# A graph network's messages: gathered before they are summed, or scattered in order of dst as they are spread

## What is computed

```python
# layer 0
msgs = edge_weight[:, None] * (h @ w)[src];   agg = segment_sum(msgs, dst)
# layer 1 (from dst to src), gate from edge attributes and node types
msg = gate * h[dst] * (cw * mj)[:, None];     agg = segment_sum(msg, src)
# layer 2, twice
x = segment_sum(x[src] * edge_weight[:, None], dst)
# layer 3, three times
prop = segment_sum(w[:, None] * h[row], col)   # w = -dis[row] * (row != col) * dis[col]
```

## Time and profile before

| what | value |
|---|---|
| median of 3 runs | 21002.24 us (20997.84 to 21006.39) |
| the profiled execution's own time | 21139.88 us |
| its span | 21138.1 us |
| busy PE / DVE / ACT / POOL | 12659.3 / 13740.0 / 5212.8 / 7402.5 us |
| DMA, mean over the span | 212 GB/s |
| written to and read from HBM | 1727.75 MB and 2805.63 MB |

### The profile page before, as it was taken

The page is one execution under the profiler, slowest core; times in us unless marked ns, Lnnn a source line. Parts: engine busy times, 40 slices in busy tenths (PEclk is TensorE's granted clock), DMA queues, the critical chain, the costliest instruction groups (busy, mean ns, idle before and its releaser), DMA issues. The chain is left out here.

```text
span 21138.1 us, 471985 instructions
## 1 busy us (share of the span) xinstructions
PE 12659.3 (60%) x138981; PEld 10558.5 (50%) x140202; DVE 13740.0 (65%) x29579; ACT 5212.8 (25%) x13806; POOL 7402.5 (35%) x7744
## 2 busy tenths in 40 slices
PE   5666666666600476557755675576556556556655
PEld 4555555555500355545544455455545545555555
DVE  8555555555533476679978876677667666666765
ACT  0222222222211354014420450153014104202400
POOL 0555555555554201533310005402520550251054
PEclk7788778788755798568888995698666666666655
DMA  7222222222255599989977896698659659866965
GB/s 275 80 81 81 81 80 81 81 81 80 78 155 120 176 343 334 333 280 340 330 228 231 279 316 182 202 322 267 183 203 407 208 160 358 309 183 237 405 185 145
DMA packets 1900227, 4491.37 MB, mean 212 GB/s; under 512 B 314350, under 2 KB 750924, under 8 KB 1899366
## 3 DMA queue, kind: packets, MB, share of 16 engines
q1 hardware_dynamic: 912598, 1942.76, 28.3%
q0 software_dynamic: 437168, 1300.53, 20.2%
q10 hardware_dynamic: 550368, 1246.92, 15.5%
HBM read 2805.63 MB, written 1727.75 MB: 214 GB/s over the span
## 5 line engine op out<-in xcount | busy, mean ns | idle before, releaser
L1435 POOL DMA_INDIRECT sum_slots<-messages,sum_rows x2820 | 2664.4, 945 | 7504.6 <-ACT sum_rows L1447 5728.8
L1518 PE MATMUL sum_sums<-sum_slots,sum_onehot 128*128 128x144 bf16 (+1 forms) x31584 | 3650.3, 298 | 2616.9 <-DVE sum_onehot L1492 1787.4
L1518 PEld LDWEIGHTS sum_sums<-sum_slots,sum_onehot 128*128 128x128 bf16 x31584 | 3193.7, 132 | 3073.4 <-issue 3073.4
L808 POOL DMA_INDIRECT records<-rec,row_i x3125 | 2992.0, 957 | 2832.8 <-DVE rec L674 2066.3
L728 PE MATMUL ps_l<-place,turned 98*128 98x98 f32 x6250 | 1158.3, 352 | 1725.7 <-ACT place L609 1719.0
L1236 PE MATMUL exp_rows<-tab,h 128*128 x40608 | 1645.6, 191 | 809.1 <-DVE exp_times L1290 500.0
L1242 PE MATMUL exp_rows<-tab,h 128*128 x13536 | 1479.5, 288 | 845.0 <-ACT exp_stage L1373 707.6
L728 PEld LDWEIGHTS ps_l<-place,turned 98*128 98x128 f32 x6250 | 1047.6, 257 | 1802.2 <-issue 1802.2
L1477 DVE TENSOR_REDUCE sum_whole<-sum_sums 128x96 f32<-128x288 f32 (+1 forms) x1974 | 914.8, 463 | 1484.7 <-remote 874.5
L1242 PEld LDWEIGHTS exp_rows<-tab,h 128*128 128x128 bf16 x13536 | 1272.0, 128 | 1052.4 <-issue 1045.2
L1236 PEld LDWEIGHTS exp_rows<-tab,h 128*128 128x128 bf16 x40608 | 1475.6, 98 | 514.8 <-issue 315.0
(11 more groups left out here) (293 smaller groups left out, 22730.8 us busy)
## 6 DMA issues: line engine op xcount, KB each, us to landing
exp_places<-src_places SPq DMA_DIRECT2D x1692, 512.0 KB, 6.1
messages<-exp_stage ACTq DMA_DIRECT2D x1410, 576.0 KB, 11.3
messages_first<-exp_stage ACTq DMA_DIRECT2D x282, 832.0 KB, 7.3
sum_slots<-messages_back SPq DMA_DIRECT2D x282, 600.0 KB, 4.4
messages_back<-fill ACTq DMA_DIRECT2D x624, 270.5 KB
l_places<-dst_places SPq DMA_DIRECT2D x282, 512.0 KB
recc<-records SPq DMA_DIRECT2D x282, 448.0 KB
l_gate<-records SPq DMA_DIRECT2D x282, 448.0 KB
```

The source lines that it names most:

```text
L808: pool.indirect_dma_start(rec_dram, bass.IndirectOffsetOnAxis(ap=row_i[:, g, k:k + 1], axis=0), rec[:, g, k, :], None).then_inc(put[g], 16)
L1435: pool.indirect_dma_start(gath[:, c, g, :], None, of_dram, bass.IndirectOffsetOnAxis(ap=row_g[:, c, g:g + 1], axis=0)).then_inc(g_dma[c], 16)
L1518: last = pe.matmul(sums[:, c % RS, g, 0:3 * width], onehot[:, c % RS, g * B + k, :], of[:, k * 3 * width:(k + 1) * 3 * width], start=(k == ...
```

## The change: what it does

Spreading no longer stores in order; summing no longer gathers. POOL scatters each group of a pair (one indirect DMA per group, L1392 of the changed kernel) to its row in the order of dst while it is spread. Blocks that hold no edge are out of range and dropped, so all three message tensors are zeroed first, in the edge stage. Summing loads rows in order on SP, and PE adds the three bf16 parts itself, by 48 matmuls of 48 columns a pair. `u_dram` is gone; its features stay in `messages_first`. In a weighted unit `less_second` moves on PE's queue to the start of the next unit.

```diff
@@ edge stage
+        zeroed = [d.rearrange("(p n) f -> p (n f)", p=P) for d in (msg0_dram, msg_dram, back_dram)]
...
                             attrs(i, first, g)
+                            sp.dma_start(*piece(i, first, g, 0)).then_inc(s_zero, 16)
...
-                            act.dma_start(to, fill[:, 0:many].bitcast(BF16)).then_inc(s_back, 16)
+                            for k in (1, 2):
+                                act.dma_start(*piece(i, first, g, k)).then_inc(s_back, 16)
@@ block stage
-                        act.copy(sent[:, c % RS, :, 0, :], f[:, :, :, D + SREL])
-                        act.copy(sent[:, c % RS, :, 1, :], f[:, :, :, D + EW])
+                        act.copy(sent[:, c % RS, :, 0:B], f[:, :, :, D + SREL])
+                        act.copy(sent[:, c % RS, :, B:2 * B], f[:, :, :, D + EW])
+                        act.copy(sent[:, c % RS, :, 2 * B], number1[:, at])
...
-                            dve.scalar_tensor_tensor(out=empty[:, :], in0=found[:, :], scalar=0.0, in1=less_big[:, :],
-                                                     op0=ALU.is_equal, op1=ALU.mult).then_inc(s_emp, 1)
-                            dve.wait_ge(s_emp, 2 * n)
-                            dve.tensor_tensor(found[:, :], found[:, :], empty[:, :], ALU.add).then_inc(s_emp, 1)
-                            dve.wait_ge(s_emp, 2 * n + 1)
-                            dve.tensor_tensor(idx_g[:, at], found[:, :], number[:, at], ALU.add).then_inc(s_fnd, 1)
@@ layer 1: the type features are read from the first message tensor
-        u_view = u_dram.rearrange("p (n f) -> p n f", f=B * G)
+        u_view = msg0_dram.rearrange("(g p) f -> p g f", p=P)[:, :, ROW // 2:ROW0 // 2]
@@ expand, PE
                                     if weighted:
+                                        if u >= 3:
+                                            less_second(i, *before(u, 3))
+                                        elif not first:
+                                            less_second(i - 1, *before(u, 3))
 
                                         pe.matmul(unread[:, :], ident_b[:, :], flat[:, 0:512], start=True, stop=True)
...
-                                        for d, step in ((2, less_first), (3, less_second)):
-                                            if u >= d:
-                                                step(i, *before(u, d))
-                                            elif not first:
-                                                step(i - 1, *before(u, d))
+                                        if u >= 2:
+                                            less_first(i, *before(u, 2))
+                                        elif not first:
+                                            less_first(i - 1, *before(u, 2))
@@ expand, ACT
-                                if c >= LAG:
-                                    store(i, c - LAG)
-                                elif not first:
-                                    store(i - 1, RC - LAG + c)
+                                if not first:
+                                    act.wait_ge(x_st[c], i * (16 * CH) + e * (TURNS * 16 * CH))
+                                act.copy(row_d[:, c, :], idx_d[:, bass.ds(i * RG + c * CH, CH)]).then_inc(x_row, 1)
@@ expand, POOL
+                                lone_wait(pool, x_row, i * RC + (e * RC * TURNS + c + 1))
+                                if weighted:
+                                    lone_wait(pool, x_third, i * UT + (bw + (c + 1) * UC))
+                                else:
+                                    for q in range(2):
+                                        lone_wait(pool, x_out[q], i * (UT // 2) + (bo + (c + 1) * (UC // 2)))
+                                for g in range(CH):
+                                    pool.indirect_dma_start(
+                                        to_dram, bass.IndirectOffsetOnAxis(ap=row_d[:, c, g:g + 1], axis=0),
+                                        stage[:, c, g, :], None,
+                                        bounds_check=last_block, oob_is_err=False).then_inc(x_st[c], 16)
@@ collect: gather (POOL), row copies (ACT) and the save of u_dram (SP) are gone
+                                sp.dma_start(slots_in[:, c, :, :],
+                                             in_order[:, bass.ds(i * RG + c * CH, CH), 0:length // 2 if wide else length]
+                                             ).then_inc(g_load[c], 16)
...
-                            dve.tensor_reduce(
-                                whole[:, :, :],
-                                sums[:, c % RS, :, 0:3 * width].rearrange("p g (j f) -> p g f j", j=3),
-                                AX.X, ALU.add).then_inc(g_red, 1)
-                            dve.wait_ge(g_red, i * RC + (bc + c + 1))
...
-                                dve.tensor_tensor(to, to, whole[:, g, :], ALU.add).then_inc(g_acc, 1)
+                                dve.tensor_tensor(to, to, sums[:, c % RS, g, 0:width], ALU.add).then_inc(g_acc, 1)
@@ collect, PE
+                                pe.matmul(unread[:, :], ident_b[:, :], places_flat[:, 0:512], start=True, stop=True)
                                 pe.wait_ge(g_oh, i * RC + (bc + c + 1))
-                                lone_wait(pe, g_dma[c], i * each + (bl + each))
+                                lone_wait(pe, g_load[c], i * 16 + (bl + 16))
                                 if c >= RS or not first:
-                                    lone_wait(pe, g_red, i * RC + (bc + c + 1 - RS))
+                                    lone_wait(pe, g_acc, i * (RC * CH) + (ba + (c + 1 - RS) * CH))
                                 for g in range(CH):
...
                                     for k in range(B):
-                                        last = pe.matmul(sums[:, c % RS, g, 0:3 * width],
-                                                         onehot[:, c % RS, g * B + k, :],
-                                                         of[:, k * 3 * width:(k + 1) * 3 * width],
-                                                         start=(k == 0), stop=(k == B - 1))
+                                        for j in range(3):
+                                            n = k * 3 + j
+                                            last = pe.matmul(sums[:, c % RS, g, 0:width],
+                                                             onehot[:, c % RS, g * B + k, :],
+                                                             of[:, n * width:(n + 1) * width],
+                                                             start=n == 0, stop=n == 3 * B - 1)
```

187 lines of the change are left out of this document (73 added, 114 removed).

## The result

The changed kernel takes **20847.25 us** (median of 4 runs, 20842.81 to 20849.54); the kernel before took 21000.04 us beside it (20997.33 to 21006.39). The ratio is 0.9927, 95% interval 0.9909 to 0.9944. It is faster, as forecast, and the time lies in the range, but of the 489 us that the sum promised 153 came.

A forecast was written before the change was run, and what follows sets the result against it. Mostly nothing was full and engines waited for each other; unweighted spreading was DMA bound. Summing -1463, weighted +734, unweighted 0, edge +250, block -50, rest +40: -489 us, 21002 to 20510 us; range 19600 to 21300.

The forecast's parts named there:

- the scatter itself fits: Weighted spreading: two scatter issues at 1.28 us take 2.55 us of POOL in a pair of 3.4.
- PE becomes the longest: Summing: PE needs 2.1 us a pair, DMA 1.9, DVE 1.66; with gaps at turns, 2.40 us a pair.
- lower bound of 1.9: Summing: at best the DMA's 1.9 us a pair, which would save 990 us more.
- rival D: Summing: gaps at PE's turns and waits overlap, 2.05 us a pair, 690 better, kernel 19820 us; chance 0.11.
- Rival B: Summing: PE's small matmuls limit at 49 ns each, 3.15 us a pair, kernel slower at 22000 us; chance 0.17.
- the loop through POOL and ACT, and the low clock that the gaps bring: Gathered summing: what the change removes, as the gather itself is not slow; pairs go from 3.25 to 2.40 us.
- The price of the order: Weighted spreading: moved less_second waits for ACT's copy, +0.75 us in one unit, +0.10 in the one with the fetch.
- rival A: Weighted spreading: the subtraction's wait falls into PE's idle time, the 734 us go, kernel 19780 us; chance 0.20.
- upper bound of 1270: Weighted spreading: at worst +1.5 us a pair, 0.75 in each unit, +1270 us.
- rival C: Unweighted spreading: scatters keep the gathers' 3.25 us a pair, three stages lose 507, kernel 21020 us; chance 0.10.
- Weighted stages hide it: Weighted spreading: scatters at the gathers' pace of 3.25 us a pair would cost nothing there.
- PE waits for `place` in 469 of 469 rounds, so all of it counts: Edge stage: ACT's second DMA delays place by 0.4 us in each of 625 rounds, +250 us.

The follow-up runs named there:

- e2: Kernel before, stores still in order on ACT's queue, with only the second subtraction moved as the change moves it: 19525.79 us, ratio 1.0569.
- e1: Changed kernel with the weighted spreading's second subtraction put back behind the 24 matmuls, on a faster chip (before: 18480 us): 17208.28 us, ratio 0.9314.
- e9: Changed kernel with the second subtraction put back behind the 24 matmuls, on a slower chip (before: 20993.81 us): 19873.37 us, ratio 0.9466.
- e8: Changed kernel with ACT's two zeroing DMAs of an edge round cut in two each, on a slower chip: 20953.65 us, edge stage 5409.8 us.
- e11: Changed kernel with PE loading spreading window numbers once per turn, not per pair, on a slower chip (before: 21133.04 us): 20977.81 us, ratio 0.9926.
- e12: Changed kernel with the second subtraction back in place and window numbers loaded once per turn, on a slower chip: 20023.69 us, ratio 0.9475.
- e5: Changed kernel with the three unweighted spreadings storing in src order from ACT instead of scattering, on a faster chip: 18006.33 us against the change's 17991.07.

## Why the prediction was wrong

The direction held, and so did the mechanisms named for the two large terms. Two steps failed. One is a cost put at nothing: "the scatter itself fits", worked out from POOL's own time. On the chip that was measured PE's signals come late beside scatters, and the six spreadings lost 2086 us where 734 were forecast. The other is a size: "PE becomes the longest" with 2.40 us a pair of the summing, where 1.95 were measured.

**Summing, -1463, measured -2347.** The miss is the pace after: (2.40 - 1.95) x 1974 pairs = 888 us. 48 matmuls take 1.22 us, not 1.64, and the stage runs at its DMA's pace, just above my lower bound of 1.9. The 34 ns of the earlier trace rows came from a stretch of 0.82 us that had the unread matmul in it. Without its 0.22, which I then added once more, it is 0.60/24 = 25 ns, what the 48 show. That is rival D's outcome, 884 us better than the forecast where I had put it at 690, though D had the gaps overlap and not the matmuls cheaper. Rival B, at 3.15 us a pair, falls. (Its threshold was also added up wrong: 3.14 - 0.49 is 2.65 us a pair, not 2.75.) The page TensorE: Matmul & The Clock Gate of the Trainium skill, section Back-to-back issue gap, gives 81 ns as the sustained spacing of pairs at 128 columns, and its table about 25 ns as the issue floor for 1 to 64 columns, which the prediction did not use. The trace, at 48 columns, has 25 ns: it agrees with the table, and the 81 ns do not carry down to them.

The pace before, 3.25, was read from the trace, so the number did not need its cause. But the cause that I gave, "the loop through POOL and ACT, and the low clock that the gaps bring", was incomplete: the same code takes 912 us on the first kind and 704 on the second, 208 us each, and ahead of its reduction DVE stands idle for 237 us in a stage of the one and 37 in one of the other. That time stood in the trace before the change, as time in which the earlier trace rows show nothing full, and I took it for the normal price of a loop. That late signals are its cause is an inference from the two kinds; no run took the gathers alone away on the first.

**Weighted spreading, +734, measured +1542.** The price of the order was sized well. On the second kind the three stages moved by +654 (3709 us against 3056 in the trace of before; they have no indirect DMA before, so the kinds should agree there). By unit it is +0.68 and +0.10 us for my +0.75 and +0.10, so rival A, by which the wait costs nothing, falls. In the kernel before, where ACT still stores, the same move costs more, 1046 for three stages (e2). What failed is "the scatter itself fits": it was true of POOL and not of those who work beside it. On the first kind both units are 1.00 us longer than before, and the +1542 are more than my upper bound of 1270. e1 and e9 separate the two: with the old order the scatters cost +597 for three stages on the first kind and -118 on the second, and the order on top of them +946 and +772.

**Unweighted spreading, 0, measured +544.** Right on the second kind (768 to 754). On the first it is the size of rival C (507), to which I gave one chance in ten, and nearly its pace (950/282 = 3.37 us for my 3.25). C carried the gathers' pace over as a pace of the queue. It is not: POOL still issues at 1.28 us within a pair; it waits for PE, ACT and DVE, and ACT waits for PE's signals (442 us a stage against 10). "Weighted stages hide it" was wrong too: the three weighted ones took 888 us more on the first kind than on the second.

**Edge stage, +250, measured -25** (and +8 on the second kind). The delay of `place` was sized right, +0.37 us for my 0.4. The step "PE waits for `place` in 469 of 469 rounds, so all of it counts" failed. A wait that ends last in every round says who was late, not that the round would end sooner: on the second kind POOL's five scatters set the round, and on the first e8 finds 0.18 us for two more issues. The sign of the -25 is not certain: set against the 5362 us of e11 and e12, whose chip is the likely one of the profile before, it would be +33. The **block stage** (-38 for -50, but +32 on the second kind) and the rest (+27 for +40) held on the chip that was measured.

**Sum.** On the second kind the terms are: summing -1174, weighted +654, unweighted -47, edge +8, block +32, the rest +53, and the total is -474, near the forecast's -489. That is luck: the summing gave 289 less than forecast, while the edge stage cost 242, the weighted stages 80 and the unweighted ones 47 less, and the block stage 82 more. On the first kind 3384 indirect DMAs moved, with their delay, out of the six gathered summings and into the six spreadings. By the difference between the kinds, the summings gained 1173 us more there, the weighted spreadings lost 888 more and the unweighted ones 591 more. So the gain given back was mostly a wait that had been there before, in another place.

The version that beats both kernels is e1: the change with the subtractions in their old order, 0.9314 of before on the second kind and 0.9466 on the first (e9).

## What to carry to other kernels

A stage in which nothing is full and everyone waits has a cause that can be read: before costing its replacement, take one signal from engine to engine (a matmul's last start and its reader's start) and compare it between stages. Here the reader came 0.04 us after the modelled end of the matmul in some places and 1.3 us after it in others, and the change moved that delay, not only the work. When two steps of one queue get a round trip through another engine between them, count that trip in full where nothing else stalls the queue (0.75 us forecast, 0.79 measured). Beside another stall give it a range: it added 0.10 us in the change and 0.44 to 0.51 in e2. Before two kernels' stages are compared, see that both ran on one chip.

## What was unexpected of the hardware

- Identical code took 20994 to 21133 us on two or three chips and 18465 to 18480 us on two others, with nearly all of the difference in stages where POOL issues indirect DMAs. Within a chip the runs of the kernel before agree to about 0.15%.
- On the slower kind, matmul signals that fall into the first 0.75 us of a scatter of the weighted spreading are answered 1.56 to 1.62 us after the scatter's start, for a scatter instruction of 0.97 us. ACT's signals there are not late (0.05 to 0.06 us), nor are DVE's in a gathered summing: PE starts 0.25 us (median) after a one-hot that ends in the first half microsecond of a gather. In the edge stage the median time from PE's last transpose to ACT's copy was 2.45 us before and 1.94 after, against 0.26 on the other kind.
- 48 pairs of weight load and matmul of 48 columns ran at 25 ns each in a stretch with granted clock 1.00, the high level (2.4 GHz).
- On the second kind the stages that store by scatter are the shorter ones: 914 against 965 us in the weighted spreading (e1), where ACT no longer issues DMAs, and 754 against 774 in the unweighted one (e5).
